# Modulation sections accumulated by chunks of the contraction in four column strips, and turned by transposes

## The chip, the cores and the metric

One core of a Trainium2 chip. The time is that of one launch on the device, in microseconds (us); the median of several executions is quoted with the lowest and the highest.

## The reference

A transformer-like block in float32 on x of 4 batches x 512 tokens x 512 features, modulated by a condition c (4 x 512):

```python
mod = (_silu(L0_c) @ L0_wmod).reshape(4, 6, 1, 512)          # L0_wmod: 512 x 3072
sa, ca, ga, sb, cb, gb = mod[:, 0], ..., mod[:, 5]
ga = (2 * (ga >= 0) - 1) * maximum(abs(ga), 0.25)            # gb likewise
h = _layernorm(x) * (1 + ca) + sa
x = x + ga * attn(h)
h = _layernorm(x) * (1 + cb) + sb
x = x + gb * ffn(h)
```

attn is a Mamba2 layer: an input projection to 3136 columns, a causal convolution of 4 taps with silu, time steps by softplus, a chunked scan over 64 heads, a gate and an output projection. ffn multiplies by weights that are reduced to their signs and a mean magnitude per output.

## The kernel before, in words

The program has a first part, a main part of 64 units (groups of heads x batches x token tiles of 128) and a tail (output projection and ffn). The change lies in the first part. Each engine has its own list of instructions, written out by hand; `start.tensor`, `start.scalar`, `start.vector`, `start.gpsimd` and `start.sync` are these lists, and engines meet at semaphores. The list of the first part runs over into the first slots of the main part (v = -2, -1), where `turn_sections`, `gate_sizes`, `mlp_columns`, `gate_values`, `gate_rows` and `gate_turn` are called.

**Modulation.** silu(c) is turned into `scT` (128 rows x 4 chunks x 32 columns, 4 used, `L491`). The six parts of mod are six sections of 512 columns of `w_mod`, taken in the order 1, 0, 4, 3, 2, 5 (`SEC`). `load_section(n)` (`L297`) brings the 512 x 512 weights of a section, 1 MB in runs of 2 KB, to one of two places in `wm`; sections 2 to 5 wait until an earlier section is done. `section(n)` (`L798`) multiplies: chunk k of the contraction goes to the rows 32k to 32k+3 of one PSUM bank, so the four partial sums of the contraction stand in four strips and are not yet added. ScalarE copies the bank to `row` (`copy_row`, `L683`). `turn_section(n)` (`L754`) then takes four products of the row's 128 columns by `pick`, a 128 x 4 matrix with ones at rows 32k+b, which adds the four strips and turns the result, so that features lie on partitions. VectorE writes scale and shift to `mod_t` (`L497` for attn, `L565` for ffn), and the gates' magnitudes and signs are made from the same bank (`L733`, `L571` to `L574`). Matrix products of float32 appear in the trace as two passes each (x8 for four products), transposes as one.

**Around it on TensorE.** Section 0, turns of x tiles 0 and 1 (`turn`, `L817`, four transposes each), transposes of the time-step weights (`L847`), section 1, turns 2 and 3, turning of sections 0 and 1, then weights and further tiles. Section 2 stands behind turn 11, section 3 behind tile projection 1 (`L1196`), sections 4 and 5 behind projection 2, ahead of turns 12 to 15 and the time-step products `dt_inputs` (`L765`). Sections 3 to 5 each wait for the copy of the row before, since they use the same bank 7. In the main part's first slots: turning of x for the scan (`L1214`), `turn_sections` with 32 passes for sections 2 to 5, `decay` (`L1205`), projections, the second `dt_inputs` and `gate_turn`, after which TensorE waits for ScalarE.

**Around it on the other engines.** ScalarE: copies of rows 0 and 1 around the copy of the time-step weights; copies 2 and 3 between the h tiles 8 to 11 (`L662`, `L666`); copies 4 and 5 behind `decays` (`L631` to `L634`) and ahead of h tile 12. In slot (-2, 2): `gate_sizes`, the exponent of the decay (`L1365`), the spread of x (`L1373`). VectorE: statistics (`L473`), normalization (`L504`), low parts, the softplus polynomial (`L586` to `L600`), scan (`L608`) and sum (`L611`), then tile 12's normalization, a low sum (`L618`), tiles 13 to 15, the convolutions (`L1446`) and silus (`L1467`), `mlp_columns`, `gate_values`, the reciprocal of the time steps (`L623`). GpSimd builds the constants (`pick` with one fill and four selects, `L384` to `L388`), takes roots (`L437`) and low parts (`L428`, `L444`).

Of the kernel before, what the change touches and what calls it, by code (L numbers as in the profile page):

```python
# [182 lines left out]
def first_part(nc, s, outer, x, w_in, conv_w, conv_b, z_bias, d_skip, cond, w_mod):  # L183
# [9 lines left out]
    pick = kept("pick", [P, NB])  # L193
# [4 lines left out]
    with ExitStack() as ctx:  # L198
        def sb(name, shape, dt=F32):
            return ctx.enter_context(nc.sbuf_tensor("p_" + name, shape, dt))  # L200

        c4, th4, row = sb("c4", [NB, D]), sb("th4", [NB, D]), sb("row", [P, 2, D])
        wa_raw, xn2, row5 = sb("wa_raw", [NH, D]), sb("xn2", [P, 2, D]), sb("row5", [P, 4, D])
        wraw, wst = sb("wraw", [P, 2, D]), sb("wst", [P, 2, 2 * P])
        stage, hf = sb("stage", [R_ALL, 2 * HG * Q]), sb("hf", [P, 2, L])
        wm = sb("wm", [P, 2, KC, D])
# [12 lines left out]
    zero_sc, picked = sem("zero_sc"), sem("picked")  # L219
# [12 lines left out]
    SEC = [1, 0, 4, 3, 2, 5]  # L232
# [38 lines left out]
    def mod_bank(n):  # L271
        return MOD[:, (n + 1) * KC * NB:(n + 2) * KC * NB]

    def row_bank(n):
        return s.bank[(7, 6, 7, 7, 7, 7)[n]]

    def row_of(n):
        return row[:, n % 2, :] if n < 4 else (s.chain[:, 1, 4, :], row5[:, 0, :])[n - 4]
# [4 lines left out]
    def sync(sp):  # L283
# [43 lines left out]
        load_section(0)  # L327
        load_section(1)
# [12 lines left out]
        load_section(2)  # L341
        load_section(3)
        load_weights(4)
        load_weights(5)
        load_section(4)
        load_section(5)
# [27 lines left out]
    def gpsimd(pool):  # L374
# [9 lines left out]
        pool.memset(pick[:, :], 0.0).then_inc(picked, 1)  # L384
        for k in range(KC):
            pool.wait_ge(picked, k + 1)
            pool.affine_select(out=pick[:, :], in_=pick[:, :], compare_op=ALU.not_equal, fill=1.0,
                               base=-32 * k, pattern=[[-1, NB]], channel_multiplier=1).then_inc(picked, 1)  # L388
# [88 lines left out]
    def vector(dve, convolve, silu):  # L477
# [16 lines left out]
        def modulation(n):  # L494

            dve.wait_ge(mod_pe, 2)
            dve.tensor_scalar(s.mod_t[:, n, :, :], mod_bank(n).rearrange("p (k b) -> p k b", k=KC),  # L497
                              1.0 - n % 2, None, ALU.add).then_inc(mod_ready, 1)
# [62 lines left out]
    def mlp_columns(dve):  # L561

        for n in (2, 3):
            dve.wait_ge(mod_pe, 6)
            dve.tensor_scalar(s.mod_t[:, n, :, :], mod_bank(n).rearrange("p (k b) -> p k b", k=KC),  # L565
                              1.0 - n % 2, None, ALU.add).then_inc(mod_ready, 1)
    def gate_values(dve):

        gt = MOD[:, 5 * KC * NB:7 * KC * NB].rearrange("p (g k b) -> p g b k", g=2, k=KC)
        dve.wait_ge(gate_abs, 1)  # L570
        dve.tensor_scalar(gs[:, :, :, :], gt, 0.0, 2.0, ALU.is_ge, ALU.mult).then_inc(gate_v, 1)  # L571
# [80 lines left out]
    def scalar(act, linear, tanh):  # L652
# [57 lines left out]
        copy_row(2)  # L710
        make_h(10)
        make_h(11)
        copy_row(3)
# [3 lines left out]
        copy_row(4)  # L717
        copy_row(5)
# [11 lines left out]
    def gate_sizes(act):  # L730

        act.wait_ge(mod_ready, 4)
        act.activation(ga[:, :, :, :], MOD[:, 5 * KC * NB:7 * KC * NB].rearrange("p (g k b) -> p g b k", g=2, k=KC),  # L733
                       ACT.Abs).then_inc(gate_abs, 1)
# [14 lines left out]
    def turn_section(pe, n):  # L749

        pe.wait_ge(sec_cp, n + 1)
        pe.wait_ge(picked, KC + 1)
        for k in range(KC):
            ins = pe.matmul(mod_bank(n)[:, k * NB:(k + 1) * NB], row_of(n)[:, k * P:(k + 1) * P], pick[:, :], start=True, stop=True)  # L754
        ins.then_inc(mod_pe, 1)

    def dt_inputs(pe, pb, q):

        wait_low(pe, 4 * (2 * pb + q) + 3)
        if (pb, q) == (1, 0):  # L760
            pe.wait_ge(sec_cp, 6)
# [8 lines left out]
    def turn_sections(pe):  # L770

        pe.wait_ge(h_act, 16)
        for n in range(2, 6):
            turn_section(pe, n)
# [8 lines left out]
    def tensor(pe, project):  # L783
# [58 lines left out]
        section(0)  # L842
# [120 lines left out]
def main_part(nc, s, outer, start, x, w_in, w_out, w_ffn, b_ffn):  # L963

    with ExitStack() as ctx:
# [78 lines left out]
        def sync(sp, tail):  # L1044
# [71 lines left out]
            sp.wait_ge(start.sec_pe, 6)  # L1116
# [925 lines left out]
```

## Time and profile before

| what | value |
|---|---|
| median of 3 runs | 672.53 us (671.93 to 673.36) |
| span of the profiled execution | 672.7 us; the page gives no other time for it |
| TensorE busy (span share) | 624.5 us (93%) |
| VectorE | 521.1 us (77%) |
| ScalarE | 379.5 us (56%) |
| GpSimd | 357.3 us (53%) |
| mean granted TensorE clock | 0.976 |
| DMA | 70.52 MB, mean 105 GB/s |

The profile is one execution. PE is TensorE, PEld its weight loads, DVE VectorE, ACT ScalarE, POOL GpSimd, SPq the queue that issues transfers. A line of the chain of waits gives start, duration and what ran there; in the order of time a bracket tells how long the engine had been idle and who released it. `L798` is line 798 of the kernel. A granted clock of 1.00 is 2.4 GHz and 0.50 is 1.2 GHz.

### The profile page before, as it was taken

The page shows a single profiled execution, that of the slowest core. Times are in us where ns is not written, and L with a number is a line of the kernel's source. Part 1 is how long each engine was busy: PE and PEld are TensorE (multiplying, and loading weights), DVE is VectorE, ACT ScalarE, POOL GpSimd, SP SyncE. Part 2 cuts the span into 40 slices and gives each one's busy share as a digit, 9 for nine tenths or more (in the row PEclk, how much of TensorE's full clock was granted, in tenths as well). Part 3 has the DMA queues.
Part 4 walks back from the last instruction along what each step waited for, and adds up shares of the span by engine and source line. Part 5 has one row for each costly group of instructions (what it writes and reads, how often), then busy time and mean ns, then how long its engine had stood idle before and what let it go on. Part 6 is the DMA issues. An engine that isn't in the chain of part 4 may idle for free.

```text
span 672.7 us, 21311 instructions
## 1 busy us (share of the span) xinstructions
PE 624.5 (93%) x8371; PEld 491.5 (73%) x8371; DVE 521.1 (77%) x947; ACT 379.5 (56%) x834; POOL 357.3 (53%) x416
## 2 busy tenths in 40 slices
PE   3887977999999999999999999999978989999995
PEld 1664756777777878778777878777866767888884
DVE  6698689888687887887778878778698466677766
ACT  3776444546646455646545564756664527665555
POOL 5674211626555463754734655447564645767652
PEclk9698889999999999999999999999997999999999
DMA  9743111242321231322122253222323634444411
GB/s 288 234 146 115 47 38 52 70 157 75 117 70 38 97 107 52 101 69 87 67 71 73 78 168 118 69 101 70 101 69 106 215 125 141 145 153 126 126 48 62
DMA packets 61914, 70.52 MB, mean 105 GB/s; under 512 B 13972, under 2 KB 33460, under 8 KB 61816
## 3 DMA queue, kind: packets, MB, share of 16 engines
q1 hardware_dynamic: 61816, 69.17, 32.1%
q8 instruction: 67, 1.10, 0.7%
q14 instruction: 31, 0.25, 0.1%
HBM read 54.45 MB, written 14.70 MB: 103 GB/s over the span
## 4 chain that ended last, share of the span: by engine, by line
PE 75%; DVE 11%; issue 4%; POOL 4%; ACT 3%; DMA 1%; SPq 0%; POOLq 0%; DVEq 0%; ACTq 0%
PE bank L1196 35%; PE bank L1962 11%; PE pair L1261 7%; PE bank L1205 4%; PE bank L1995 3%; PE pair L1234 3%; PE bank L1291 2%; DVE m_cv L1446 2%; PE bank L1214 2%; PE pair L1247 2%; POOL h_lo L428 1%; DVE chain L589 1%; DVE chain L596 1%; DVE m_M L1476 1%; PE pair L1274 1%
## 5 line engine op out<-in xcount | busy, mean ns | idle before, releaser
L1446 DVE SCALAR_TENSOR_TENSOR m_cv<-bank,gpc,m_cv 128x511 f32<-128x511 f32 (+2 forms) x192 | 143.4, 747 | 38.3 <-ACT m_cv L1353 33.6
L1196 PE MATMUL bank<-h_hi,w_hi 128*128 128x512 f32 x384 | 164.6, 429 | 3.6 <-DVE m_xs L1467 1.9
L1196 PE MATMUL bank<-h_hi,w_lo 128*128 128x512 f32 x384 | 153.1, 399 | 0.0
L1196 PE MATMUL bank<-h_lo,w_hi 128*128 128x512 f32 x384 | 152.5, 397 | 0.4 <-issue 0.4
L1353 ACT ACTIVATE m_cv<-bank,gpc 128x512 f32<-128x512 f32 x96 | 72.0, 750 | 79.8 <-PE bank L1196 79.4
L1365 ACT ACTIVATE m_M<-bank 128x512 f32<-128x512 f32 x128 | 76.0, 594 | 66.5 <-PE bank L1205 65.3
L1591 POOL TENSOR_TENSOR m_S<-m_S,m_cd 128x128 f32<-128x128 f32 x96 | 40.0, 416 | 136.9 <-DVE m_S L1509 71.3
L1196 PEld LDWEIGHTS bank<-h_hi,w_hi 128*128 128x128 f32 x384 | 74.0, 193 | 24.4 <-issue 5.5
L1581 POOL TENSOR_TENSOR m_Xw<-m_Xp,wend 128x256 f32<-128x256 f32 x64 | 39.8, 622 | 87.7 <-ACT m_Xp L1373 87.7
L1196 PEld LDWEIGHTS bank<-h_hi,w_lo 128*128 128x128 f32 x384 | 73.4, 191 | 17.5 <-issue 0.6
L1196 PEld LDWEIGHTS bank<-h_lo,w_hi 128*128 128x128 f32 x384 | 73.9, 192 | 12.1 <-issue 0.3
L1476 DVE TENSOR_TENSOR m_M<-m_M,pair 128x512 f32<-128x512 f32 x128 | 81.7, 679 | 0.2 <-issue 0.2
L1261 PEld LDWEIGHTS pair<-m_M,m_Xp 64*32 64x32 f32 x4096 | 45.7, 105 | 25.9 <-issue 25.5
L1261 PE MATMUL pair<-m_M,m_Xp 64*32 64x64 f32 x4096 | 56.3, 225 | 7.9 <-DVE m_M L1476 7.9
L1360 ACT ACTIVATE bank<-m_cv 128x512 f32<-128x512 f32 x96 | 58.4, 608 | 6.3 <-DVE m_cv L1446 6.3
L1816 POOL TENSOR_TENSOR t_y_lo<-h_lo_place,t_y_hi 128x1024 fp32r<-128x1024 f32 x16 | 39.1, 2445 | 39.6 <-ACT t_y_hi L1762 35.1
L1205 PE MATMUL bank<-R,Lm 84*128 84x512 f32 x128 | 57.3, 448 | 1.5 <-ACT m_M L1365 1.5
L1962 PE MATMUL bank<-h_hi,t_y_hi 128*128 128x512 f32 x128 | 51.5, 403 | 1.3 <-POOL t_y_lo L1816 1.3
L1962 PE MATMUL bank<-h_hi,t_y_lo 128*128 128x512 f32 x128 | 50.7, 396 | 0.0
L1962 PE MATMUL bank<-h_lo,t_y_hi 128*128 128x512 f32 x128 | 50.7, 396 | 0.0
L1467 DVE SCALAR_TENSOR_TENSOR m_gate<-bank,m_cv 128x512 f32<-128x512 f32 x32 | 22.1, 690 | 33.3 <-ACT bank L1360 33.3
L1602 POOL TENSOR_TENSOR m_t<-m_xs,m_dd 128x512 f32<-128x512 f32 x32 | 40.6, 1291 | 4.0 <-DMA m_dd<-dd_scratch 3.1
(184 smaller groups left out, 1260.0 us busy)
## 6 DMA issues: line engine op xcount, KB each, us to landing
m_ea<-ea_scratch SPq DMA_DIRECT2D x32, 256.0 KB
m_dd<-dd_scratch SPq DMA_DIRECT2D x32, 256.0 KB
y_scratch<-m_t SPq DMA_DIRECT2D x16, 512.0 KB, 3.4
h_lo_place<-y_scratch SPq DMA_DIRECT2D x16, 512.0 KB, 4.7
p_wm<-in_L_wmod_dram SPq DMA_DIRECT2D x6, 1024.0 KB, 6.9
m_wraw<-in_L_attn_in_proj_w_dram SPq DMA_DIRECT2D x18, 256.0 KB, 3.1
w_lo_place<-in_L_attn_input__dram SPq DMA_DIRECT2D x16, 256.0 KB, 4.9
out_dram<-t_o SPq DMA_DIRECT2D x16, 256.0 KB, 2.4
```

Source lines behind the costliest of these rows:

```text
L1196: ins = pe.matmul(A[k % 3][:, :], w[:, t, kc, :], h[:, n % NB, kc, :], start=(m == 0), stop=(m == 11))
L1205: pe.matmul(DB[:, :], s.Lm[:, u % 2, q, :], s.R[:, u % 2, q, :], start=True, stop=True).then_inc(d_done, 1)
L1261: ins = pe.matmul(YS[32 * j:32 * j + 32, c, q * Q:(q + 1) * Q], Xp[half, u % 2, HG * q + h, :], M[half, u % 2, q, h * Q:(h + 1) * Q], star ...
L1353: act.activation(cv[:, k % 3, :], A[k % 3][:, :], ACT.Identity, scale=scale, bias=bias).then_inc(lin_done, 1)
L1360: act.activation(A[k % 3][:, :], cv[:, k % 3, :], ACT.Tanh).then_inc(tanh_done, 1)
L1365: act.activation(M[:, u % 2, q, :], DB[:, :], ACT.Exp).then_inc(exp_done, 1)
L1446: ins = dve.scalar_tensor_tensor(out=cv[:, k % 3, lag:], in0=A[k % 3][:, 0:L - lag], scalar=s.gpc[:, gp, o:o + 1], in1=cv[:, k % 3, lag:], ...
L1476: dve.tensor_tensor(m, m, g, ALU.mult).then_inc(m_done, 1)
L1581: pool.tensor_tensor(Xw[:, :, :].rearrange("p q (j e d) -> p (q j) e d", e=2, d=HD), src, w, ALU.mult).then_inc(xw_done, 1)
L1591: pool.tensor_tensor(S1[:, c, :].rearrange("p (h d) -> p h d", h=HG), S[:, (m - 1) % 4, :].rearrange("p (h d) -> p h d", h=HG), cd[:, b // ...
L1602: pool.tensor_tensor(t1[:, q, :], xs[:, n % 2, q, :], dd[:, q, :], ALU.mult).then_inc(t1_done, 1)
L1962: ins = pe.matmul(OB[i][:, :], y[:, i, k, :], w[k], start=(k == 0 and m == 0), stop=(k == KI - 1 and m == 2))
```

## The change

The weights are brought and multiplied in another cut. For attn's shift and scale (columns 0 to 1023 of `w_mod`) two loads bring two chunks of the contraction each (runs of 4 KB); `early_sections` takes, for each chunk, four products of 256 columns, one to each strip of bank 7, and accumulates the four chunks there. For the other four parts (columns 1024 to 3071) four loads bring one chunk each (runs of 8 KB), and `late_sections(k)` takes four products of 512 columns, one to each strip, accumulating over k. So a strip holds finished values of its own columns. One copy of 256 columns and one of 512 replace the six, and `turn_rows` takes two, later four, 128 x 128 transposes in place of picking products; the readers of the turned bank get other views. `pick` goes. Products 0 and 1 both stand where section 1 stood; the waits on copies between the late sections go. The diff:

```diff
+    wm_late = wm.rearrange("p (r j) d -> p r (j d)", r=2)
+    MODA = MOD[:, P:3 * P]
+    def early_columns(sec):
+        return MODA.rearrange("p (i c j r) -> p c j i r", i=2, c=2, j=2)[:, sec, :, :, 0:NB]
+    def late_columns(sec):
+        return MOD.rearrange("p (k c r) -> p c k r", k=KC, c=4)[:, sec - GA, :, 0:NB]
+    def gate_columns():
+        return MOD.rearrange("p (k c r) -> p c r k", k=KC, c=4)[:, 0:4:3, 0:NB, :]
...
-        def load_section(n):
-            if n >= 2:
-                sp.wait_ge(sec_pe, n - 1)
-            sp.dma_start(wm[:, n % 2, :, :], wmv[:, :, SEC[n] * D:(SEC[n] + 1) * D]).then_inc(d_wm[n % 2], 16)
+        def load_early_rows(i):
+            sp.dma_start(wm[:, 2 * i:2 * i + 2, :], wmv[:, 2 * i:2 * i + 2, 0:2 * D]).then_inc(d_wm[i], 16)
+        def load_late_rows(k):
+            sp.wait_ge(sec_pe, max(k, 1))
+            sp.dma_start(wm_late[:, k % 2, :], wmv[:, k, 2 * D:6 * D]).then_inc(d_wm[k % 2], 16)
...
-        pool.memset(pick[:, :], 0.0).then_inc(picked, 1)
-        for k in range(KC):
-            pool.wait_ge(picked, k + 1)
-            pool.affine_select(out=pick[:, :], ...).then_inc(picked, 1)
...
-            dve.wait_ge(mod_pe, 2)
+            dve.wait_ge(mod_pe, 1)
...
-        def copy_row(n):
-            act.wait_ge(sec_pe, n + 1)
-            if n in (2, 3):
-                act.wait_ge(mod_pe, n - 1)
-            act.activation(row_of(n), row_bank(n)[:, :], ACT.Copy).then_inc(sec_cp, 1)
+        def copy_rows(late):
+            act.wait_ge(sec_pe, 5 if late else 1)
+            cols = slice(0, D if late else 2 * P)
+            act.activation(row[:, late, cols], DTB[:, cols], ACT.Copy).then_inc(sec_cp, 1)
...
-        copy_row(0)
         act.wait_ge(wa_pe, 1)
...
-        copy_row(1)
+        copy_rows(0)
...
         make_h(9)
-        copy_row(2)
         make_h(10)
         make_h(11)
-        copy_row(3)
         linear(1)
         linear(2)
         decays(act, 0)
-        copy_row(4)
-        copy_row(5)
+        copy_rows(1)
...
-    def turn_section(pe, n):
-        pe.wait_ge(sec_cp, n + 1)
-        pe.wait_ge(picked, KC + 1)
-        for k in range(KC):
-            ins = pe.matmul(mod_bank(n)[:, k * NB:(k + 1) * NB], row_of(n)[:, k * P:(k + 1) * P], pick[:, :], start=True, stop=True)
+    def turn_rows(pe, late):
+        pe.wait_ge(sec_cp, 1 + late)
+        dst = MOD if late else MODA
+        for k in range(KC if late else 2):
+            ins = pe.transpose(dst[:, k * P:(k + 1) * P], row[:, late, k * P:(k + 1) * P], s.ident[:, :])
         ins.then_inc(mod_pe, 1)
...
-        def section(n):
-            pe.wait_ge(d_wm[n % 2], 16 * (n // 2 + 1))
-            if n == 2:
-                pe.wait_ge(w_act, 10)
-            if n >= 3:
-                pe.wait_ge(sec_cp, n)
-            for k in range(KC):
-                ins = pe.matmul(row_bank(n)[32 * k:32 * k + 32, :], scT[:, k, :], wm[:, n % 2, k, :], start=True, stop=True)
+        def early_sections():
+            for k in range(KC):
+                if k % 2 == 0:
+                    pe.wait_ge(d_wm[k // 2], 16)
+                for j in range(4):
+                    ins = pe.matmul(DTB[32 * j:32 * j + 32, 0:2 * P], scT[:, k, :], wm[:, k, j * 2 * P:(j + 1) * 2 * P],
+                                    start=(k == 0), stop=(k == KC - 1))
+            ins.then_inc(sec_pe, 1)
+        def late_sections(k):
+            pe.wait_ge(d_wm[k % 2], 16 * (k // 2 + 2))
+            if k == 0:
+                pe.wait_ge(w_act, 10)
+            for j in range(4):
+                ins = pe.matmul(DTB[32 * j:32 * j + 32, :], scT[:, k, :], wm_late[:, k % 2, j * D:(j + 1) * D],
+                                start=(k == 0), stop=(k == KC - 1))
             ins.then_inc(sec_pe, 1)
...
         pe.wait_ge(cond_step, 4)
-        section(0)
         turn(0)
         turn(1)
...
-        section(1)
+        early_sections()
         turn(2)
         turn(3)
-        pe.wait_ge(sec_cp, 2)
-        turn_section(pe, 0)
-        turn_section(pe, 1)
+        turn_rows(pe, 0)
...
-        section(2)
+        late_sections(0)
         project(1, 0)
         project(1, 1)
-        section(3)
+        late_sections(1)
         project(2, 0)
         project(2, 1)
-        section(4)
-        section(5)
+        late_sections(2)
+        late_sections(3)
```

## Rows read from the trace of the kernel before

**Rows 1.** The page: the chain that ended last, by engine
```profile
PE 75%; DVE 11%; issue 4%; POOL 4%; ACT 3%; DMA 1%; SPq 0%; POOLq 0%; DVEq 0%; ACTq 0%
```

**Rows 2.** The chain from 15 to 21 us: start, us, what
```profile
15.29 1.86 PE pair L798 x8
17.16 1.90 PE bank L817 x8
19.06 1.81 PE pair L754 x16
```

**Rows 3.** The order of time, 50 to 60 us, with waits in brackets
```profile
50.28 1.06 PE L798 MATMUL pair<-p_wm,p_scT 128*32 128x512 f32 x8 [1.45 <-ACT p_row L683]
...
56.74 1.49 DVE L504 TENSOR_SCALAR p_xn<-chain,p_mv,p_rstd 128x512 f32<-128x512 f32 x1
...
59.25 1.11 PE L798 MATMUL pair<-p_wm,p_scT 128*32 128x512 f32 x8 [3.95 <-ACT chain L683]
59.82 1.45 DVE L504 TENSOR_SCALAR p_xn<-chain,p_mv,p_rstd 128x512 f32<-128x512 f32 x3
```

**Rows 4.** The chain from 60 to 92 us
```profile
60.36 0.83 PE bank L817 x3
...
73.59 3.47 PE pair L754 x32
...
80.00 0.43 PE bank L1205
...
82.08 2.81 PE pair L765 x12
...
86.87 0.45 PE pair L1247 x8
...
91.09 0.76 DVE m_cv L1446
```

**Rows 5.** The order of time, TensorE's turns of raw weights: start, us, instruction
```profile
21.29 0.63 PE L837 MATMUL pair<-ident,p_wraw 128*128 128x128 f32 x4 [0.44 <-DVE mod_t L497]
...
25.45 1.08 PE L837 MATMUL bank<-ident,p_wraw 128*128 128x128 f32 x4
```

**Rows 6.** Busy time by stretch: TensorE, its loads, VectorE, ScalarE, GpSimd; clock; DMA
```profile
22.60:32.80 10.20, 8.04 (x26) 6.33 (x27) 6.98 (x13) 9.61 (x18) 9.67 (x11) 0.50 0.97 347
60.10:63.50 3.40, 3.40 (x19) 3.21 (x16) 3.33 (x7) 0.60 (x1) 0.00 (x0) 0.51 0.46 160
63.50:77.20 13.70, 12.01 (x72) 9.97 (x71) 9.32 (x15) 9.05 (x17) 6.05 (x5) 1.00 0.20 62
77.20:80.60 3.40, 3.40 (x10) 2.58 (x9) 0.62 (x5) 1.52 (x4) 0.62 (x1) 0.50 0.00 0
```

**Rows 7.** Section 0's passes (line 798, 10.4 to 11.1 us): ns min/median/max, starts
```profile
L798 PE MATMUL pair<-p_wm,p_scT x8: 1031/1061/1062, 10.1 to 11.0; 128*32 128x512 f32 x8
```

**Rows 8.** Turns 8 to 11 alone (line 817): stretch, then TensorE busy (instructions)
```profile
42.98:44.83 1.85, 1.84 (x16) 1.68 (x16) 1.00 0.01 4
```

**Rows 9.** The load issued at 51.4 us (tile p_wm)
```profile
DMA to landing us min/median/max: 5.1/5.1/5.1
```

**Rows 10.** The order of time, 74 to 88 us
```profile
74.93 0.69 DVE L1467 SCALAR_TENSOR_TENSOR m_Ct<-bank,m_cv 128x512 f32<-128x512 f32 x1
...
77.09 0.25 DVE L565 TENSOR_SCALAR mod_t<-pair 128x16 f32<-128x16 f32 x2 [1.48 <-PE pair L754]
...
77.54 0.59 ACT L1365 ACTIVATE m_M<-bank 128x512 f32<-128x512 f32 x1
...
80.85 2.32 DVE L1446 SCALAR_TENSOR_TENSOR m_cv<-bank,gpc,m_cv 128x511 f32<-128x511 f32 x3 [2.67 <-ACT m_cv L1353]
...
87.57 0.29 DVE L1506 COPY m_S<-pair 128x128 f32<-128x128 f32 x1 [0.62 <-PE pair L1274]
```

**Rows 11.** The order of time, GpSimd's first instructions
```profile
2.18 1.19 POOL L387 TENSOR_SCALAR_AFFINE_SELECT p_pick<-p_pick 128x4 f32<-128x4 f32 x4
...
5.02 1.40 POOL L393 TENSOR_SCALAR_AFFINE_SELECT p_stage<-p_stage 64x1024 f32<-64x1024 f32 x1 [1.65 <-DVE p_chunk_on L484]
```

More of the change, by code:

```diff
@@ L192, in first_part @@
     scT, st, mv, rstd = kept("scT", [P, KC, 32]), kept("st", [P, 16, 6]), kept("mv", [P, 16, 2]), kept("rstd", [P, 16, 2])
-    pick = kept("pick", [P, NB])
     half, dcol, cde = kept("half", [P, 1]), kept("dcol", [P, 1]), kept("cde", [P, 2, NC])
@@ L218, in first_part @@
     sec_pe, sec_cp = sem("sec_pe"), sem("sec_cp")
-    zero_sc, picked = sem("zero_sc"), sem("picked")
+    zero_sc = sem("zero_sc")
     gate_abs, gate_v, gate_pe, gate_ready = sem("gate_abs"), sem("gate_v"), sem("gate_pe"), sem("gate_ready")
@@ L231, in first_part @@
     a_skip = sem("a_skip")
-    SEC = [1, 0, 4, 3, 2, 5]
+    SA, CA, GA, SB, CB, GB = range(6)
     start = Shared()
@@ L269, in hf_of @@
         return (hf, hf2)[n % 4 // 2][:, n % 2, :]
[L271 to L278, printed above, removed]
+    wm_late = wm.rearrange("p (r j) d -> p r (j d)", r=2)
[6 more added lines that the diff above has]
+        return MOD.rearrange("p (k c r) -> p c r k", k=KC, c=4)[:, 0:4:3, 0:NB, :]
     def w_bank(n):
@@ L326, in sync @@
             load_x(i)
-        load_section(0)
-        load_section(1)
+        load_early_rows(0)
+        load_early_rows(1)
         sp.dma_start(wa_raw[:, :], w_in[2 * DI + 2 * NG * NS:, :]).then_inc(d_wa, 16)
@@ L340, in sync @@
         load_weights(3)
-        load_section(2)
-        load_section(3)
+        load_late_rows(0)
+        load_late_rows(1)
         load_weights(4)
         load_weights(5)
-        load_section(4)
-        load_section(5)
+        load_late_rows(2)
+        load_late_rows(3)
     def store_decays(sp, pb):
@@ L383, in gpsimd @@
         pool.memset(scT[:, :, :], 0.0).then_inc(zero_sc, 1)
-        pool.memset(pick[:, :], 0.0).then_inc(picked, 1)
-        for k in range(KC):
-            pool.wait_ge(picked, k + 1)
-            pool.affine_select(out=pick[:, :], in_=pick[:, :], compare_op=ALU.not_equal, fill=1.0,
-                               base=-32 * k, pattern=[[-1, NB]], channel_multiplier=1).then_inc(picked, 1)
         def constant_shapes():
@@ L494, in modulation @@
         def modulation(n):
-            dve.wait_ge(mod_pe, 2)
-            dve.tensor_scalar(s.mod_t[:, n, :, :], mod_bank(n).rearrange("p (k b) -> p k b", k=KC),
+            dve.wait_ge(mod_pe, 1)
+            dve.tensor_scalar(s.mod_t[:, n, :, :].rearrange("p (j i) b -> p j i b", j=2), early_columns((CA, SA)[n]),
                               1.0 - n % 2, None, ALU.add).then_inc(mod_ready, 1)
@@ L563, in mlp_columns @@
         for n in (2, 3):
-            dve.wait_ge(mod_pe, 6)
-            dve.tensor_scalar(s.mod_t[:, n, :, :], mod_bank(n).rearrange("p (k b) -> p k b", k=KC),
+            dve.wait_ge(mod_pe, 2)
+            dve.tensor_scalar(s.mod_t[:, n, :, :], late_columns((CB, SB)[n - 2]),
                               1.0 - n % 2, None, ALU.add).then_inc(mod_ready, 1)
     def gate_values(dve):
-        gt = MOD[:, 5 * KC * NB:7 * KC * NB].rearrange("p (g k b) -> p g b k", g=2, k=KC)
         dve.wait_ge(gate_abs, 1)
-        dve.tensor_scalar(gs[:, :, :, :], gt, 0.0, 2.0, ALU.is_ge, ALU.mult).then_inc(gate_v, 1)
+        dve.tensor_scalar(gs[:, :, :, :], gate_columns(), 0.0, 2.0, ALU.is_ge, ALU.mult).then_inc(gate_v, 1)
         dve.tensor_scalar(ga[:, :, :, :], ga[:, :, :, :], 0.25, None, ALU.max).then_inc(gate_v, 1)
@@ L732, in gate_sizes @@
         act.wait_ge(mod_ready, 4)
-        act.activation(ga[:, :, :, :], MOD[:, 5 * KC * NB:7 * KC * NB].rearrange("p (g k b) -> p g b k", g=2, k=KC),
-                       ACT.Abs).then_inc(gate_abs, 1)
+        act.activation(ga[:, :, :, :], gate_columns(), ACT.Abs).then_inc(gate_abs, 1)
     def gate_rows(act):
@@ L760, in dt_inputs @@
         if (pb, q) == (1, 0):
-            pe.wait_ge(sec_cp, 6)
+            pe.wait_ge(sec_cp, 2)
         first = 64 - 64 * q
@@ L772, in turn_sections @@
         pe.wait_ge(h_act, 16)
-        for n in range(2, 6):
-            turn_section(pe, n)
+        turn_rows(pe, 1)
     def gate_turn(pe):
@@ L1115, in sync @@
             load_chunk_decays(0)
-            sp.wait_ge(start.sec_pe, 6)
+            sp.wait_ge(start.sec_pe, 5)
             load_scales(0)
```

4 lines of the change are left out of this document (2 added, 2 removed).

## The prediction

> **What bounds the kernel now.** I read the page first, then the chain of waits stage by stage, then the order of time around each piece of the change. TensorE holds 75% of the chain over the whole span [rows 1]: from about 120 us on it is the bound, and the change touches nothing there. So a gain in the first 90 us counts in full if it moves the point at which that stage begins. What bounds the four places where the modulation stands:
>
> - 15 to 21 us: section 1, turns 2 and 3, and the picking products of both sections follow one another on TensorE [rows 2]; the two mod_t writes wait for them.
> - 21 to 59 us: GpSimd's low parts, then VectorE's softplus polynomial and scan. TensorE is off the chain.
> - 55 to 64 us: ScalarE's four decays, its copy of row 4, section 5 on TensorE, which had sat idle 3.95 us for that copy [rows 3], and four turns [rows 4].
> - 72 to 91 us: 32 picking passes, then decays, projections and time-step products on TensorE, then ScalarE. From 91.09 the chain is nearly all VectorE's until 120 us, beginning with the taps [rows 4]; it takes over any shift.
>
> **The clock.** Four turns of raw weights took 0.63 us at 21.29 and 1.08 at 25.45 [rows 5]. The second lies where the granted clock was 0.50, that is 1.2 GHz (22.6 to 32.8); it was so again from 60.1 to 63.5 and from 77.2 to 80.6, and 2.4 GHz between these [rows 6]. Section 0's passes took 1.06 us each at 10.1 us [rows 7] where eight of them take 1.06 in all at 50.28 [rows 3]. So TensorE was at the low level at 10 us and at the high one by 21.
>
> **Part 1, sections 0 and 1.** Before, four products go to four column strips, two passes each; the second four passes begin 0.86 us after the first [rows 7], and section 1 takes 1.86 us [rows 2]. After, 16 products of 256 columns (32 passes) replace 8 of 512 (16 passes): the same columns, again four strips at a time. I take two sections' time, 2 times 1.86 = 3.7 us, now all of it after 15.29, where section 1 stood; it ends at 19.0 and not 17.15. Section 0 was off the chain, so taking it away gives nothing back. Turns 2 and 3 (eight transposes) cost 1.90 us low [rows 2], or half of 1.85 = 0.92 high (16 transposes [rows 8]). The 16 picking passes, 1.81 us [rows 2], become two transposes, 0.23 high, 0.46 low. The single copy of 256 columns lies beside the turns, as the copy at 17.2 did. High: 19.0 + 0.92 + 0.23 = 20.15 against 20.87, 0.7 gained. Low: 19.0 + 1.90 + 0.46 = 21.4, 0.5 lost. The clock stood high by 21 after just such an unbroken run, so I take a value near the high end, 0.4 gained, and keep both ends. Whatever it is goes on in full: mod_t starts ScalarE's h, GpSimd's low parts, the next roots and so VectorE's chain.
>
> **Part 2, ScalarE's copies and the last sections.** Copies 2 and 3 go (0.6 us each) and so do the waits on them: section 3 stood 1.45 us for copy 2 [rows 3], so TensorE is that much early there. VectorE holds the chain beside it, so this is worth 0, except that the last load goes out before 51.4; it took 5.1 us [rows 9], so it lands by 56.5. Section 5 waited for copy 4, behind the decays, until 59.25; the last chunk waits for its load alone and is done by 57.6. Late next is the input of the turns: xn of tile 12 at 58.23, tiles 13 to 15 from 59.82 at 0.48 each, after VectorE's low sum [rows 3]. Turn 12 then runs by itself; turns 13 to 15 start at 60.3 as the four did before. At the low level a turn is 0.85 us (three transposes 0.64, one 0.21; 0.83 for the first three [rows 4]), so they end at 62.9 against 63.8: **0.95 gained**. At the high level the last input binds at 61.3 and the gain is 1.9; that is the other bound. TensorE is even idler before 60 than it was when the clock fell, so I take 0.95. Copies 4 and 5 become one, 0.6 us beside these turns; if the turns did not cover it, it would stand ahead of h on ScalarE. The shift goes on through h, tanh 0 and silu 0 to projection 3.
>
> **Part 3, the turns of the late sections.** The 32 picking passes take 3.47 us [rows 4]; four transposes take 0.46 high, 0.85 low. All 0.95 earlier, turning x ends at 72.65, the four transposes at 73.1, the first decay at 73.35 and six projection passes at 74.75. Now a wait appears that was covered: the second decay needs ScalarE's exponent of the first; ahead of that on ScalarE stands the size of the gates, which needs the two late mod_t writes, which stand behind silu 3 on VectorE. silu 3 ended at 75.62 [rows 10], now 74.67; mod_t at 74.95; from the end of mod_t (77.34) to that of the exponent (78.13) the rows show 0.8 [rows 10]; so the decay goes at 75.8 against 80.0 [rows 4]. Behind it, up to the 12 time-step products, come a decay, a turn and six passes, 2.08 us before [rows 4], partly low; 1.75 high (0.23 + 0.11 + six at 0.235). Then the products, 2.81, and ScalarE's 1.98 before TensorE goes on at 86.87 [rows 4]: now 82.3, 4.55 earlier. On VectorE the taps of tile 4 wait for ScalarE, which does that tile's bias behind the exponent (75.75) and the spread (0.4): 0.8 more, taps at 76.95 against 80.85, 3.9 earlier. The reciprocal and the scaling behind them end 3.9 earlier too, and the copy of the state, which had waited 0.62 at 87.57 [rows 10], goes 4.5 earlier. Bias and taps of tile 5 (91.09) follow. **Parts 2 and 3 together give 4.5**, 0.95 and 3.55.
>
> **Edits at nothing.** GpSimd's five instructions on pick (1.3 us) lie ahead of 1.65 us of waiting for VectorE's constants [rows 11]; without that cover they would be worth 1.3. The loads carry the same six megabytes in runs of 4 and 8 KB, not 2: section 1 followed the transposes without a gap at 15.29, so its load was there, and the last is covered by xn until 58.2 (1.7 us of slack). SP has nothing behind them until the decays at 57.6. The readers of mod_t and the gates take as many columns as before, 0.12 us each in the pair [rows 10]. Buffers made after pick lie 16 bytes lower: no row shows what that does, the nearest is nothing, and I keep 0.5 us either way.
>
> **Sum.** 0.4 + 0.95 + 3.55 = 4.9. The profiled execution's span is 672.7 us, 0.2 above the median 672.53; no other time is given for it. 672.7 - 4.9 = 667.8, or 667.6 from the median: **667.7 us**.
>
> **Rivals.**
> (a) The clock falls in part 3 all the same. For it: TensorE gets a gap of 1.05 us before 75.8; it fell at 77.2 though marked busy since 73.6, with 32 tiny products. Against it: it stayed high from 63.5 to 77.2 with 1.7 us idle [rows 6]. A low stretch of 3.4 us costs 1.7: gain 3.2, 669.5 us. Chance 0.15.
> The Trainium skill (TensorE: Matmul & The Clock Gate, Part 4: PE-mode transpose) says that transposes do not keep the clock up as products do. The low stretch from 22.6, mostly transposes, agrees; by that rule the result would be this rival's.
> (b) Part 1 at the low level: 0.5 lost, not 0.4 gained: 668.6 us. Chance 0.13.
> (c) A wait that I did not follow ends last before 91 us and eats half of part 3. VectorE was idle 4.4 us of 63.5 to 77.2 and 2.8 of the next 3.4 [rows 6], so not by its work, by order only: gain 2.5, 670.2. Chance 0.08.
> (d) Slower: the four strips stop running side by side, since four products share a chunk and the next four accumulate onto them. Then early_sections takes 32 passes at 0.43 (half of 0.86), 13.8 against 3.7: 10 us more, all on the chain, 672.7 + 10 - 4.5 = 678 us. It decides from 1.0 us for a group of four passes on (0.43 expected). Against it: four strips overlapped before. Chance 0.05.
> (e) Nothing arrives: 672.5. Chance 0.04.
> (f) More: turns 13 to 15 at the high level, part 1 at its high end: 0.95 + 0.3, 666.5 us. Chance 0.10.
> The forecast itself, 667.0 to 668.5: 0.45.
>
> **Numbers.** The range 666.0 to 670.3 takes in the forecast, (a), (b), (c) and (f), 0.9 of the chance, with the bounds of part 1 and of the buffers' places; without (c) it would be less sure than is asked. A measurement here can tell about 0.2%, 1.3 us, from no change: faster 0.91, same 0.04, slower 0.05.
>
> **What would show it.** mod_t near 20.3; 32 passes within 4 us after 15.3; the last chunk over by 57.6 and a lone turn 12; the late turns in 0.5 us; the second decay released by the exponent at 75.5; granted clock 1.00 between 73 and 80; taps near 86.2 in place of 91.09. A group of four passes over 1 us, or those taps moved by less than 3 us, would make it wrong.

## The result, and the profile after the change

The changed kernel takes 668.05 us (median of 6 runs, 665.93 to 669.14) against 672.23 us before on the same chip (6 runs, 670.38 to 673.36): a ratio of 0.9933, with a 95% interval from 0.9914 to 0.9953. The forecast was 667.7 us with a range from 666.0 to 670.3, and "faster" with a chance of 0.91. The profiled execution took 668.28 us; its span is 666.5.

From the page of the changed kernel: the span, the engines, the granted clock and the chain by engine.

```profile
span 666.5 us, 21236 instructions
...
PE 617.1 (93%) x8345; PEld 485.4 (73%) x8345; DVE 520.8 (78%) x947; ACT 377.2 (57%) x830; POOL 356.5 (53%) x411
...
PEclk9897998999999999999999999999997999999999
...
PE 76%; DVE 12%; issue 4%; POOL 4%; ACT 3%; POOLq 0%; DVEq 0%; ACTq 0%
```

TensorE's share of the chain is nearly what it was (76% against 75% in [rows 1]); the instructions that the change touches stand in the first 86 us. Its pieces stand in the chain that ended last (start, length, what; lines that answer to [rows 2] and [rows 4]):

```profile
12.76 1.94 PE bank L821 x8
14.70 0.62 PE bank L850 x4
15.32 3.57 PE pair L791 x32
18.89 1.17 PE bank L821 x8
20.06 0.23 PE pair L750 x2
...
20.41 0.05 DVE mod_t L500
...
59.84 0.90 PE bank L821 x3
...
74.44 0.17 DVE mod_t L568 x2
...
74.69 0.10 ACT p_ga L730
74.79 0.59 ACT m_M L1366
...
75.43 0.50 PE bank L1206
...
77.43 2.76 PE pair L761 x12
...
82.17 0.45 PE pair L1248 x8
...
85.94 0.67 DVE m_cv L1447
```

The reader should see five things. The 32 passes of the first two sections take 3.57 us, so the four column strips still overlap. Two transposes of 0.23 us stand where 16 picking products took 1.81 [rows 2]. The late picking products, 3.47 us [rows 4], have gone from the chain. In their place stands a wait that was not on the chain before: from 74.44 to 75.43 the chain runs through mod_t, the gates and ScalarE's exponent before the second decay (L1206) may start. And the taps of tile 5 begin at 85.86 (the chain joins them at 85.94), where they began at 91.09 [rows 4].

The order of time around the late chunks and turns shows the waits in brackets (these answer to [rows 3] and [rows 10]):

```profile
52.12 1.06 PE L801 MATMUL pair<-p_wm,p_scT 128*32 128x512 f32 x8
54.30 1.06 PE L801 MATMUL pair<-p_wm,p_scT 128*32 128x512 f32 x8 [1.11 <-DMA p_wm<-in_L_wmod_dram]
57.70 0.90 PE L821 MATMUL bank<-ident,p_xn 128*128 128x128 f32 x3 [2.34 <-DVE p_xn L507]
57.94 0.58 ACT L684 ACTIVATE p_row<-pair 128x512 f32<-128x512 f32 x1
59.84 0.90 PE L821 MATMUL bank<-ident,p_xn 128*128 128x128 f32 x3 [1.03 <-DVE p_xn L507]
72.24 0.60 PE L750 MATMUL pair<-ident,p_row 128*128 128x128 f32 x4
74.35 0.24 DVE L568 TENSOR_SCALAR mod_t<-pair 128x16 f32<-128x16 f32 x2
75.43 0.50 PE L1206 MATMUL bank<-R,Lm 84*128 84x512 f32 x1 [0.97 <-ACT m_M L1366]
82.87 0.29 DVE L1507 COPY m_S<-pair 128x128 f32<-128x128 f32 x1 [0.42 <-PE pair L1275]
85.86 2.31 DVE L1447 SCALAR_TENSOR_TENSOR m_cv<-bank,gpc,m_cv 128x511 f32<-128x511 f32 x3
```

The last chunk is released by its load at 54.30, no longer by ScalarE at 59.25 [rows 3]; then the turn of tile 12 waits for its normalization, as do the other three. Busy time by stretch, with the granted clock after the five engines (columns as in [rows 6]):

```profile
56.80:63.60 6.80, 4.88 (x19) 4.29 (x20) 6.71 (x9) 2.56 (x7) 1.97 (x2) 0.50 0.34 119
63.60:77.20 13.60, 11.38 (x53) 8.55 (x53) 10.01 (x19) 10.49 (x22) 6.67 (x6) 1.00 0.19 63
77.20:80.60 3.40, 3.09 (x15) 2.19 (x13) 3.36 (x3) 0.38 (x1) 0.00 (x0) 1.00 0.00 0
...
494.00:525.00 31.00, 26.53 (x447) 21.11 (x448) 22.77 (x49) 16.85 (x39) 18.19 (x22) 0.78 0.43 129
```

The clock is at the low level (0.50, that is 1.2 GHz) over the late turns, as it was before, and at the high one from 63.6 through 80.6, where before it fell at 77.2 [rows 6]. From 494 to 525 us it is 0.78 here and 0.83 in the first trace of the kernel before; these low stretches come back below.

**Where the time came from**, by marks of the same work in both traces (us from the start of the span):

```
                                        before   after   gained so far
first mod_t of the attention part        20.89   20.32     0.6
normalization of tile 12                 56.74   56.15     0.6
end of the turn of tile 15               63.8    62.7      1.2
taps of tile 5                           91.09   85.86     5.2
taps of tile 16                         171.6   167.0      4.7
last taps                               499.1   493.9      5.1
end of the span                         672.7   666.5      6.2
```

### The profile page after: what moved, and what is told of

The parts are those of the page before. It is cut to its first block, busy times and chain, and to the rows that moved or that the text cites. A ratio compares the mean times of both kernels' runs of the same rounds, so it can differ in the third digit from the quotient of the medians.

```text
span 666.5 us, 21236 instructions
## 1 busy us (share of the span) xinstructions
PE 617.1 (93%) x8345; PEld 485.4 (73%) x8345; DVE 520.8 (78%) x947; ACT 377.2 (57%) x830; POOL 356.5 (53%) x411
## 4 chain that ended last, share of the span: by engine, by line
PE 76%; DVE 12%; issue 4%; POOL 4%; ACT 3%; POOLq 0%; DVEq 0%; ACTq 0%
PE bank L1197 35%; PE bank L1963 11%; PE pair L1262 7%; PE bank L1206 4%; PE bank L1996 3%; PE pair L1235 3%; PE bank L1292 2%; DVE m_cv L1447 2%; PE bank L1215 2%; PE pair L1248 2%; DVE m_M L1477 1%; PE pair L1275 1%; POOL h_lo L431 1%; DVE chain L591 1%; DVE chain L598 1%
## 5 line engine op out<-in xcount | busy, mean ns | idle before, releaser
L1447 DVE SCALAR_TENSOR_TENSOR m_cv<-bank,gpc,m_cv 128x511 f32<-128x511 f32 (+2 forms) x192 | 143.3, 747 | 35.2 <-ACT m_cv L1354 30.7
L1817 POOL TENSOR_TENSOR t_y_lo<-h_lo_place,t_y_hi 128x1024 fp32r<-128x1024 f32 x16 | 39.0, 2440 | 38.6 <-ACT t_y_hi L1763 34.1
L1206 PE MATMUL bank<-R,Lm 84*128 84x512 f32 x128 | 57.0, 445 | 2.5 <-ACT m_M L1366 2.5
```

Of the source, the lines that this page charges most:

```text
L1206: pe.matmul(DB[:, :], s.Lm[:, u % 2, q, :], s.R[:, u % 2, q, :], start=True, stop=True).then_inc(d_done, 1)
L1447: ins = dve.scalar_tensor_tensor(out=cv[:, k % 3, lag:], in0=A[k % 3][:, 0:L - lag], scalar=s.gpc[:, gp, o:o + 1], in1=cv[:, k % 3, lag:], ...
```

## Experiments

Each kernel was timed against the kernel before on the same chip. Two marks are quoted throughout: the normalization of tile 12 ("tile 12") and the taps of tile 5 ("taps"). Before they are 34.4 us apart, after 29.7; the difference of 4.6 is what the second and third parts are worth, free of what happened ahead of them, but with whatever the granted clock did in between.

**The late part alone.** The kernel before, with chunks and transposes for the four late sections only; sections 0 and 1 with their picking products stay.

```
+ load_late_rows(0); load_late_rows(1); ...      - load_section(2) ...
+ late_sections(0..3)                            - section(2) ... section(5)
+ 4 transposes of row[:, 1, :] into MOD          - turn_section(pe, 2..5)
  (early sections, their copies and picks unchanged)
```

> The kernel before with the late part of the change alone: sections 0 and 1 stay as they were, the other four parts come by chunks and are turned by four transposes. My theory (the three parts add up): mod_t for attn stays near 20.9 us, the taps of tile 5 come at 86.4 to 86.6 instead of 91.1, and the time is 4.2 to 4.7 us below the kernel before, about 667.8. Rival (the early part carries a good share, or it is what keeps the clock up later): less than 3.5 us below, above 668.7, with taps at 87.5 or later.

Measured: 668.67 us, ratio 0.9929 (0.9905 to 0.9953). Tile 12 at 57.7, taps at 87.4. The stretch is 29.7 us, exactly the changed kernel's. The place was missed by 0.8 to 1.0 us, for a reason that stands ahead of the late sections: in this execution the granted clock was 0.50 from 35.0 to 41.8, which the first traces of the kernel before and of the changed kernel do not show, and tile 12 came 37.4 us behind mod_t, not 35.8. The trace is that of the slowest of five executions (670.49 us). By the medians, 4.2 us below the kernel before on this chip (672.89), nearly the whole gain in time is here.

**The early part alone.** The kernel before, with the first two sections in 16 products of 256 columns and two transposes; the late sections stay whole.

```
- section(0); ...; section(1)          + early_sections()   (after turn(1))
- turn_section(pe, 0), (pe, 1)         + 2 transposes of row[:, 0, 0:256]
```

> The kernel before with the early part alone: columns 0 to 1023 by chunks of 256 columns per strip, one copy, two transposes; sections 2 to 5 with picking products as before. My theory: mod_t at 20.3 us instead of 20.9, everything up to 91 us 0.5 earlier, time 0.5 us below the kernel before (671.7), not to be told from no change by the times, only by the trace. Rival (the early part is worth nothing or loses, as at the low clock): mod_t at 20.9 to 21.4 and 672.2 to 672.8.

Measured: 671.99 us, ratio 0.9994 (0.9967 to 1.002). mod_t at 20.4 and tile 12 at 56.2 are 0.5 earlier than before, but the turn of tile 15 ends at 64.0 (63.8 before) and the taps stand at 91.3 (91.09), where 0.5 us earlier was expected. The 0.5 us was given back between: the granted clock was 0.50 from 56.8 on, not from 60.1 as before [rows 6], so section 5 ran in 1.93 us at 58.73 where it took 1.11 [rows 3]. In the changed kernel nothing of that length waits there, since its last chunk is over by 55.4. So in this one trace, one of the slowest of ten executions (676.35 us, with a median of 671.99), the early part kept nothing of its 0.5 us. That it keeps it together with the late part is seen in the changed kernel's traces up to tile 12; no time here is sharp enough to show it.

**The picking products put back.** The changed kernel, with 28 more passes of four columns ahead of the four late transposes; their results are overwritten.

```
         if late:
+            for k in range(14):
+                pe.matmul(MOD[:, 4*k:4*k+NB], row[:, 1, (k % KC) block], s.ident[:, 0:NB], ...)
```

> The changed kernel with 28 tiny passes (14 products of 128 x 4) put ahead of the four late transposes, so that TensorE spends about 3 us more there, as before the change. My theory (these passes stood on the path): the new wait for the exponent is 1 us long, so 2.0 us of the 3.0 arrive, and if the granted clock falls behind them as it did before, 1.7 more: taps of tile 5 at 88 to 90 against 85.9, time 2 to 3.7 us above the changed kernel, 670 to 671.7. Rival (they were covered, the gain came through the waits on copies): within 0.7 us of the changed kernel, taps near 86.

Measured: 671.63 us, ratio 0.9976 (0.9952 to 0.9999). The order of time in its trace:

```profile
72.31 3.19 PE L751 MATMUL pair<-ident,p_row 128*128 128x4 f32 x28
75.35 0.63 PE L753 MATMUL pair<-ident,p_row 128*128 128x128 f32 x4
75.74 0.51 PE L1209 MATMUL bank<-R,Lm 84*128 84x512 f32 x1
...
77.46 0.40 PE L1209 MATMUL bank<-R,Lm 84*128 84x512 f32 x1
```

And its busy time by stretch:

```profile
77.20:80.60 3.40, 3.40 (x17) 2.72 (x16) 2.06 (x3) 1.57 (x4) 0.62 (x1) 1.00 0.00 0
```

The passes take 0.114 us each (3.19 / 28). The second decay now has no wait and starts at 77.46 against 75.43, and the taps are at 87.8, 1.9 later: 3.2 us of added passes less the wait of 1.0 that they cover. That is the trade that the forecast's third part describes, run backwards. In this execution the clock stayed at 1.00 from 77.2 to 80.6 although the tiny products were back. It was one of the fastest of ten, 668.42 us, where the median lies 3.6 above the changed kernel's (2.9 by the ratios) and not 1.9. The expectation had 1.7 us more for the case that the clock falls behind the passes; whether it fell in the slower executions no trace shows.

**The old wait put back.** The changed kernel, with TensorE held ahead of the last chunk until ScalarE has done the four decays, as section 5 was.

```
         late_sections(2)
+        pe.wait_ge(a_act[0], B_WE)
         late_sections(3)
```

> The changed kernel with TensorE waiting for ScalarE's four decays before the last late chunk, so that this chunk stands where section 5 stood, ahead of turn 12. My theory: turns 12 to 15 end 0.9 us later (63.3 against 62.4), and all of it is handed on to the taps of tile 5, time 0.9 above the changed kernel, about 669.0. Rival (turns are bound by their inputs in either order): turns end within 0.3 us of the changed kernel's, no difference in the time.

Measured: 669.76 us, ratio 0.9947 (0.993 to 0.9964). The stretch is 30.7 us (30.65), 0.9 longer than with the change (29.71), as expected:

```profile
58.77 1.93 PE L801 MATMUL pair<-p_wm,p_scT 128*32 128x512 f32 x8 [3.86 <-ACT chain L636]
...
60.63 0.90 PE L821 MATMUL bank<-ident,p_xn 128*128 128x128 f32 x3
60.76 0.60 ACT L684 ACTIVATE p_row<-pair 128x512 f32<-128x512 f32 x1 [2.05 <-PE pair L801]
```

The chunk stands in front of all four turns and takes 1.93 us at the low level; with the change the turn of tile 12 is over before the others' input is there. In the kernel before, section 5 had taken only 1.11 us in this place, nearly all of it at the high level [rows 3], so this run returns more than the change had taken away: 0.9 us, where the two first traces differ by 0.6 at the end of the late turns.

**The changed kernel once more**, beside the next three, to see its spread.

> The changed kernel once more, for its spread beside the others on one chip. My theory (what is left after the three parts is where the granted clock falls, which differs from execution to execution): from tile 12's normalization to the taps of tile 5 it takes 29.7 us as before within 0.3, while mod_t stands anywhere from 19.2 to 20.4 and the span differs by up to 3 us from the first profile; median 667.5 to 668.7. Rival (the shift of 5.2 at the taps and 6.2 at the end belongs to the change): span 666.5 within 0.5.

Measured: 667.53 us (7 runs, 665.25 to 669.69), ratio 0.9919 (0.9883 to 0.9956). All marks up to the last taps agree with the first trace within 0.3 us (taps 85.8, last taps 493.6), but the span is 663.6, 2.9 us shorter. What differs is the clock from 494 to 525 us, 0.94 here and 0.78 in the first trace of the changed kernel. So the span moves by 2.9 us with nothing changed. The clock does not explain, though, why the first two spans lie 1.0 us further apart than their last taps (6.2 against 5.1): there the kernel before had the higher clock, 0.83 against 0.78. From the last taps to the first h of the ffn in the tail the three traces without the late part take 57.0, 58.1 and 59.5 us, the eleven with it 54.3 to 57.0. Whether that is chance or something that the change does behind 494 us stays open.

**The gates' size behind the first exponent.** This takes away the new wait before the second decay.

```
-                    if (v, sl) == (-2, 2):
-                        start.gate_sizes(act)
 ...
                         exponent(u, 0)
                         spread(u)
+                        if v == -2:
+                            start.gate_sizes(act)
```

> The changed kernel with the size of the gates put behind the exponent and the spread on ScalarE, so that the second decay no longer waits for silu 3 and the late mod_t. My theory (that wait, 0.97 us on TensorE, is now on the path): the second decay goes at its place with under 0.2 us of waiting, the taps of tile 5 come 0.6 to 0.9 us earlier counted from tile 12's normalization (28.9 instead of 29.7), time 0.7 below the changed kernel. Rival (VectorE is the bound by then): the decay goes earlier but the taps stay, no difference.

Measured: 667.05 us, ratio 0.9908 (0.9877 to 0.9939).

```profile
73.26 0.58 ACT L1366 ACTIVATE m_M<-bank 128x512 f32<-128x512 f32 x1
73.89 0.19 PEld L1206 LDWEIGHTS bank<-R,Lm 84*128 84x128 f32 x1 [0.25 <-ACT m_M L1366]
73.90 0.49 PE L1206 MATMUL bank<-R,Lm 84*128 84x512 f32 x1
74.24 0.20 ACT L730 ACTIVATE p_ga<-pair 128x32 f32<-128x32 f32 x1
```

The exponent no longer stands behind p_ga, the decay's wait of 0.97 is gone but for 0.25 on its weight load, and the stretch falls from 29.7 to 28.6 us, 0.3 more than expected. The time is 0.5 us below the changed kernel's on the same chip, which these intervals cannot tell from nothing.

**The early sections in two halves.** Two of the four chunks go ahead of turn 0, where TensorE had been idle waiting for tile 0; the other two stay behind the raw weights.

```
-        def early_sections():
-            for k in range(KC):
+        def early_sections(half):
+            for k in range(2 * half, 2 * half + 2):
 ...
+        early_sections(0)
         turn(0)
 ...
-        early_sections()
+        early_sections(1)
         turn(2)
```

> The changed kernel with the first two chunks of the early product put back ahead of turn 0, where section 0 stood and TensorE was idle, and only the other two where they are. My theory (the move of section 0 onto the path costs 1.8 us of the 2.4 that the transposes give back): mod_t 0.9 us earlier at the same moment of the clock's rise (19.4 for a rise at 19.2, 18.4 for one at 17), handed on to VectorE's chain, time 0.9 below the changed kernel. Rival (the first load is not there at 10 us, or GpSimd's root binds): mod_t within 0.3 of 20.3.

Measured: 665.18 us (4 runs, 663.88 to 667.07), ratio 0.988 (0.9827 to 0.9934). The order of time in its trace:

```profile
10.79 1.93 PE L791 MATMUL pair<-p_wm,p_scT 128*32 128x256 f32 x16 [4.74 <-DMA p_wm<-in_L_wmod_dram]
12.67 1.97 PE L822 MATMUL bank<-ident,p_xn 128*128 128x128 f32 x8
...
15.27 1.67 PE L791 MATMUL pair<-p_wm,p_scT 128*32 128x256 f32 x16
...
18.61 0.22 DVE L500 TENSOR_SCALAR mod_t<-pair 128x16 f32<-128x16 f32 x2
```

The first half costs nothing: turn 0 starts at 12.67 as ever. mod_t is at 18.6 against 20.3, but tile 12 only 0.8 us earlier (55.4 against 56.2). In this trace the chain from 15.38 to 19.06 no longer passes through mod_t; it runs through the weights' low part, VectorE's statistics (p_st, p_mv) and GpSimd's root. So about half of the step was handed on and the rest met the next wait. Part of it is not the edit's at all: the clock rose at 16.5 us here and at 19.2 in the first trace of the changed kernel. The changed kernel's early part with the rise at 16.8 and 17.0 (the old wait put back, the matrix built again) has mod_t at 19.2 and 19.3, so the halves are worth some 0.6 us at mod_t, not 0.9. The stretch is 29.7, unchanged.

**Both of these together.**

> Both edits together. My theory: they add up, 1.6 us below the changed kernel and 6 below the kernel before, about 666.3. Rival (what is gained ahead of 59 us is given back as the clock falls earlier on an idler TensorE, as in the run of the early part alone): 0.7 us below the changed kernel or less, 667.4 or more.

Measured: 666.23 us, ratio 0.99 (0.9863 to 0.9937). The taps are at 83.4, against 85.1 with the halves alone, yet the lead of 1.7 shrinks: 0.9 at tile 16 (164.6 against 165.5), 0.4 at the last taps (492.2 against 492.6). The time does not show it.

**GpSimd's small matrix built again.** The changed kernel, with pick allocated and its five instructions put back, unused.

```
+    pick = kept("pick", [P, NB])
 ...
+        pool.memset(pick[:, :], 0.0) ...; 4 x pool.affine_select(out=pick[:, :], ...)
```

> The changed kernel with the picking matrix kept and built by GpSimd as before, unused: this undoes the removal of five GpSimd instructions and the shift of the later buffers by 16 bytes, and nothing else. My theory (both are worth nothing): GpSimd's first select on the stage starts at 5.0 us either way, the stretch from tile 12's normalization to the taps of tile 5 takes 29.7 us, time within the changed kernel's own spread, 667 to 669. Rival (the buffers' places matter): durations of VectorE's 128 x 512 instructions or of the loads differ by over 1%, time off by 1 us or more.

Measured: 667.14 us (5 runs, 664.63 to 667.31), ratio 0.9904 (0.9872 to 0.9935), within the spread of the changed kernel; stretch 29.8. GpSimd's 1.3 us and the 16 bytes by which later buffers move were rightly put at nothing.

**The kernel before once more.**

> The kernel before once more, for its profile. My theory (the distance of 6.2 between the two spans is 4.5 to 5 of the change and the rest the clock's place near 500 us): taps of tile 5 at 90.4 to 91.6, 34.4 from tile 12's normalization on within 0.5, but a span that differs from 672.7 by up to 2.5. Rival: span 672.7 within 0.5 and the same low stretches of the clock.

Measured: 672.17 us, span 670.4, 2.3 less than in its first trace. The stretch is 34.6, as expected, but the taps stand at 89.7, ahead of the 90.4 to 91.6 that were expected. The reason is in TensorE's order of time:

```profile
14.60 1.06 PE L798 MATMUL pair<-p_wm,p_scT 128*32 128x512 f32 x8
15.60 1.10 PE L817 MATMUL bank<-ident,p_xn 128*128 128x128 f32 x8
16.53 1.85 PE L754 MATMUL pair<-p_pick,p_row 128*128 128x4 f32 x16
```

The same passes took 1.86 us and the same turns 1.90 by the chain in [rows 2] (1.93 and 1.97 in the order of time): here the clock had risen at 13.7 us, there at 19.2 (the first record of the granted clock begins at the rise, and the lengths change with it). mod_t of the unchanged kernel was at 18.4 instead of 20.9.

**The two best versions repeated**, beside the last two.

> The first half of the early product ahead of turn 0, again, for a firm time. My theory: 0.9 to 1.7 below the changed kernel (668.05 and 667.53 in two sessions), 666.2 or a little less; ratio to the kernel before 0.989 to 0.991. Rival: the 665.18 of four executions holds, ratio 0.988 or less.

> Both edits again. My theory: the taps of tile 5 come 1.6 to 1.8 earlier than with the split alone at the same moment of the clock's rise, and the time is below the split's by up to 1 us, ratio 0.988 to 0.990. Rival (a shift gained before 91 us is lost around 500 us, where the clock falls): no difference to the split alone.

Measured: 665.97 us (6 runs), ratio 0.9897 (0.9867 to 0.9927) for the halves; 666.32 us (6 runs), ratio 0.9899 (0.986 to 0.9939) for both. The marks repeat within 0.2 us (18.5, 55.3, 85.0 and 18.5, 54.6, 83.2). The halves are the version to keep: on the same chip they lie 2.3 us below the changed kernel (665.18 against 667.53) and 1.2 below the changed kernel with its unused matrix (665.97 against 667.14), though the intervals overlap; the second edit adds nothing measurable on top.

## Why the prediction was right, step by step

**Part 1** was taken at +0.4 between 0.7 and -0.5, and measured 0.57 (mod_t 20.32 against 20.89). Its terms: 32 passes 3.7 forecast, 3.57 measured; turns 2 and 3 between 0.92 and 1.90, measured 1.17, nearly all at the high level; two transposes 0.23, measured 0.23. Rival (b) did not happen. The clock rose at 19.2 in both traces, so the comparison is fair. With the same moment of rise, the turns had moved from in front of it to behind it. The forecast took its value from the unbroken run that ended at 21; it did not know the moment of the rise, which differs by over 5 us between executions, so that the value came near is in part luck. A second pair agrees: new early part with the rise at 18.2 (gates' size behind), mod_t 19.9; old early part with the rise at 17.9 (late part alone), 20.3. The step that did not hold is the sentence that this part "goes on in full": it does in the changed kernel, but the early part alone gave it back before 64 us.

**Part 2** was taken at 0.95. The last chunk was over at 55.4 (forecast: by 57.6), turn 12 ran alone, and the others ended at 62.7, 1.2 earlier, 0.6 of it from part 1. That reading gives 0.6; putting the old wait back gives 0.9, with its chunk at the low level. So the mechanism was right and the term was taken 0.4 too large. Most of what is missing lies in the size of the turns: three of them took 2.83 us (59.84 to 62.67) where 3 times 0.85 = 2.55 was taken from rows of turns that followed others. The high bound, 1.9, needed the high clock; a low stretch covered at least a part of these turns in every one of the 14 traces.

**Part 3** was taken at 3.55. The wait named in advance appeared where it was put: the second decay went at 75.43, released by the exponent, behind p_ga, behind mod_t, behind silu 3. Forecast was 75.8 without part 1's share. Returning the passes (1.9 later) and removing the wait (1.1 earlier) shows both ends of the step.

Parts 2 and 3 together were 4.5 in the forecast and are 4.6 by the stretch from tile 12 to the taps (34.35 to 29.71), but this agreement hides two errors. At the copy of the state (87.57 before, 82.87 after) the gain counted from tile 12 is 4.1: 0.6 of part 2 and 3.5 of part 3, as forecast. The taps gained 0.5 more than that, and the forecast has no term for it. The kernel before had a second low stretch of the clock, from 87.4 to 90.9, over the six projection passes that ScalarE and the taps wait for; the forecast priced only the one from 77.2 to 80.6. Two lines of its chain and a stretch (columns as in [rows 6]):

```profile
77.44 2.56 PE bank L1196 x6
...
87.43 2.82 PE bank L1196 x6
...
85.00:91.00 6.00, 4.13 (x26) 3.32 (x27) 4.29 (x7) 2.99 (x6) 0.41 (x1) 0.72 0.04 11
```

After the change six such passes take 1.40 and the clock is 1.00 from 85 to 91:

```profile
76.04 1.40 PE bank L1197 x6
...
85.00:91.00 6.00, 6.00 (x111) 4.70 (x110) 5.79 (x10) 2.97 (x7) 1.00 (x2) 1.00 0.21 63
```

So 0.4 too much in part 2 and 0.5 from a low stretch that the forecast had not priced cancel by luck. The same rows tell how much of the 4.6 us is the clock at all. With the passes put back and the clock high, 1.72 us lie between the starts of the two decays (75.74 and 77.46) and 10.3 from there to the taps; in the kernel before it was 2.88 (76.92 and 79.80) and 11.3. That is 2.1 us of low clock, beside 1.9 of passes and 0.6 of part 2. The forecast counted on a high clock behind the transposes and put 1.7 us on its rival (a); of the 4.6 us measured, nearly half hangs on it.

Does the change keep the clock up? All three traces with the old late part (the kernel before twice and the early part alone) have low stretches that begin at 77.2, 75.1 and 77.3 and again at 87.4, 85.4 and 87.5. Of the eleven with the new one, none has a low stretch that begins between 66 and 84 us, and one has the second (the old wait put back, from 85.0). So the clock's share goes with the late part. Which of its edits brings it is not shown: neither the passes nor the wait alone brought the fall at 77 back, in one trace each, and both together were not tried.

**Edits at nothing** stayed at nothing, by the run with the matrix kept and by the load that landed 1.1 us into TensorE's idle time at 54.30, 3.4 us before anybody else needed TensorE.

**The sum** was 4.9; at the taps it is 5.2 and at the last taps 5.1. In medians it is 4.2 against the first six executions of the kernel before, 5.0 on the second chip, and 6.2 for the changed kernel with its unused matrix on the third (667.14 against 673.34). The forecast measured it against one profiled execution of span 672.7. In every run listed the span lies 1.7 to 1.9 us below the run's own time, so that execution's time would be some 674.5 by the same difference, against the median of 672.53: the step "the span is 0.2 above the median" compared two different quantities. It did no harm, since 4.9 taken from the median gives nearly the same, 667.6.

**Rivals.** (a), a low stretch in part 3, did not occur: the granted clock was 1.00 from 63.6 to 107.9. The Trainium skill (TensorE: Matmul & The Clock Gate, Part 4: PE-mode transpose) says that transposes do not keep the clock up; here four of them are 0.60 us among projections, and the trace gives that rule nothing to act on. Against the rule's reading in the forecast: by time only about half of TensorE's work from 22.6 to 32.8 was transposes (18 of 26 instructions, 4.8 of 10.0 us added up), and 16 of them in a row ran at the high level [rows 8]. Whether the fall at 77.2 before was owed to the 32 tiny products stays open, as said above. For it: the three traces with them fell there. Against it: with 28 such passes put back the clock stayed at 1.00 in the one execution that was traced. (c), an unseen wait, did not occur; its price was also wrong in the forecast, since half of part 3 is 1.8, which leaves a gain of 3.1 and 669.6 us, not 2.5 and 670.2. (d), strips one after another, would have needed 1.0 us for four passes; they took 0.45 (3.57 / 8). (e) is excluded by the interval. (f), 666.5, is the span of the profiled run by accident only; neither of its two conditions was met in full. One reading under "The clock" compares two different things: section 0's single passes (1.06 us each, overlapped) with eight passes together (1.06). Eight together took 1.94 us at 10.14 and 1.06 at 50.28, which carries the same conclusion.

## What to carry to other kernels

Price a removed piece by following the engine past it to the next wait: here 3.2 us of passes were worth 1.9 us and not 3.2, since a wait of 1.0 us stood behind them, and part 3 came out because that wait was worked out ahead of time. When the kernel before has low stretches of the clock behind that place, give each its own term: here they were worth 2.1 us of 4.6. Work on an idle engine in front of a known start (half of the early sections ahead of turn 0) cost nothing here, but its gain ends where the second-longest chain stands. And compare kernels by the distance between two marks of the same work, not by their spans, when an execution can differ from the next by as much as the change is worth.

## What the runs showed of the hardware that was not expected

- The moment at which the clock first rises differs between executions of one kernel (13.7 and 19.2 us for the kernel before) and moves mod_t by 2.5 us. By the taps 1.4 us of it is left (89.7 against 91.1), by the last taps 1.2 (497.9 against 499.1); that the spans differ by 2.3 has the clock around 500 us in it too (0.94 and 0.83 from 494 to 525).
- A low stretch of 6.8 us near 35 us came in three of the 14 traces (35.0, 34.1 and 33.8), and in these tile 12 stands 37.4 to 37.7 us behind mod_t, against 35.8 to 35.9 in the traces of the changed kernel. Later ones begin between 75 and 141 us and between 494 and 521, in varying number. Over the executions of the changed kernel the mean granted clock roughly follows the time: 0.987 with 665.93 and 665.45, 0.973 with 668.79; one run at 0.978 took 669.69.
- A pass of four columns takes 0.114 us at the high level, a transpose of 128 columns about the same (0.60 us for four, with the first one's latency). The weight loads of such passes go at the same pace (16 of them in 1.86 us, 0.116 each, at 73.31 in the kernel before). Between 4 and 128 moving columns the time did not grow.
- A lead of 1.7 us at 83 us shrank to 0.4 by the last taps in both runs of the version with both edits. A low stretch at 105.3 against 95.0 is one difference between those traces; what eats the lead was not tried.
